# P times V in quarter-width tiles, a chain's items in a row, shift in place, 64-row mask products, merged constant loads, idle transposes first

## The reference

```python
q, k, v = (proj(Wq), proj(Wk), proj(Wv))
scores = einsum('bhsd,bhtd->bhst', q, k) * scale
scores = where(mask[None, None, :, :], -inf, scores)
out = einsum('bhst,bhtd->bhsd', softmax(scores), v).transpose(0, 2, 1, 3).reshape(B, S, E) @ Wo.T
xn = out / rms(out) * rms_scale
x = x + xn * (1.0 + sc[:, None, :]) + shift[:, None, :]      # sc, shift from silu(cond) @ Wc.T + bc
...
x = x + attention(g1 * x * inv_rms(x) + b1)                  # layer 1, no mask
x = x + (silu(n @ gate.T) * (n @ hid.T)) @ out_w.T           # n = g2 * x * inv_rms(x) + b2
```

## Time and profile before

| | |
|---|---|
| median of three runs | 370.43 us |
| profiled execution | 367.09 us |
| its span, first to last instruction | 365.3 us |
| TensorE matmul busy | 348.2 us, 95% |
| VectorE busy | 225.7 us, 62% |
| ScalarE busy | 216.0 us, 59% |
| GpSimd busy | 130.9 us, 36% |
| chain that ended last, by engine | PE 80%, DVE 7%, issue 3%, ACT 3% |

### The profile page before, as it was taken

How to read it: one execution, slowest core, us unless ns; L and a number is a source line. 1 busy time by engine, 2 the same in 40 slices (tenths; PEclk the granted TensorE clock), 3 DMA queues, 4 the chain that set the end, 5 groups by cost and what they waited for, 6 DMA issues and landing times.

```text
span 365.3 us, 10610 instructions
## 1 busy us (share of the span) xinstructions
PE 348.2 (95%) x4402; PEld 328.9 (90%) x4402; DVE 225.7 (62%) x361; ACT 216.0 (59%) x462; POOL 130.9 (36%) x146
## 2 busy tenths in 40 slices
PE   3899989899999999999999999999999999998995
PEld 3698889789999989998999999999999999998994
DVE  2377973979358878458356575766675765447241
ACT  4388878889866657256644647555684554442230
POOL 3005475953144213351037141334224216034422
PEclk9899999999999999999999999999999999999999
DMA  5738325300120000200020000000000000000001
GB/s 154 249 117 240 115 74 190 116 3 31 24 95 2 2 4 2 88 29 4 2 87 31 2 3 31 2 2 3 2 31 2 3 2 31 1 2 2 29 11 48
DMA packets 11919, 16.98 MB, mean 46 GB/s; under 512 B 1728, under 2 KB 6112, under 8 KB 11872
## 3 DMA queue, kind: packets, MB, share of 16 engines
q1 hardware_dynamic: 11872, 16.31, 14.2%
HBM read 14.14 MB, written 2.16 MB: 45 GB/s over the span
## 4 chain that ended last, share of the span: by engine, by line
PE 80%; DVE 7%; issue 3%; ACT 3%; SPq 2%; POOL 2%; DMA 1%; POOLq 0%; ACTq 0%; DVEq 0%
PE ps L1433 56%; PE ps L1531 8%; PE ps L1517 7%; PE ps L1507 4%; DVE row_max L1044 2%; PE ps L1542 2%; PE ps L1563 2%; PE ps L1496 2%; SPq L291 1%; DVE shifted L1052 1%; DVE xs_row L1097 1%; ACT v_pairs L594 1%; POOL h_lo L433 1%; DMA mask_u<-in_mask 1%; ACT probs L604 1%
## 5 line engine op out<-in xcount | busy, mean ns | idle before, releaser
L433 POOL TENSOR_TENSOR h_lo<-w_stage,h_hi 128x512 fp32r<-128x512 f32 x32 | 41.2, 1289 | 105.5 <-ACT h_hi L664 105.2
L1433 PE MATMUL ps<-ff_hi,w_hi 128*128 128x256 f32 x256 | 73.6, 288 | 0.1
L1433 PE MATMUL ps<-ff_hi,w_lo 128*128 128x256 f32 x256 | 72.1, 282 | 0.0
L1433 PE MATMUL ps<-ff_lo,w_hi 128*128 128x256 f32 x256 | 72.0, 281 | 0.0
L1044 DVE TENSOR_REDUCE row_max<-ps 128x8 f32<-128x512 f32 x64 | 43.7, 682 | 14.8 <-PE ps L1507 14.8
L604 ACT ACTIVATE probs<-shifted 128x512 f32<-128x512 f32 x64 | 39.4, 631 | 17.7 <-DVE shifted L1052 17.2
L1433 PEld LDWEIGHTS ps<-ff_hi,w_hi 128*128 128x128 f32 x256 | 48.2, 188 | 0.6 <-issue 0.5
L1433 PEld LDWEIGHTS ps<-ff_lo,w_hi 128*128 128x128 f32 x256 | 48.2, 188 | 0.0
L1433 PEld LDWEIGHTS ps<-ff_hi,w_lo 128*128 128x128 f32 x256 | 48.2, 188 | 0.0
L1433 PE MATMUL ps<-in_hi,w_hi 128*128 128x256 f32 x128 | 39.1, 306 | 6.5 <-DVE w_lo L1033 5.5
L1052 DVE SCALAR_TENSOR_TENSOR shifted<-row_max,ps 128x512 f32<-128x512 f32 x64 | 43.9, 687 | 2.2
(11 more groups left out here) (88 smaller groups left out, 803.6 us busy)
## 6 DMA issues: line engine op xcount, KB each, us to landing
w_stage<-in_weights SPq DMA_DIRECT2D x20, 256.0 KB, 3.4
mod_tile<-mod_rows_dram SPq DMA_DIRECT2D x32, 128.0 KB, 3.1
x_T<-in_xT SPq DMA_DIRECT2D x8, 256.0 KB, 2.7
x_row<-in_x SPq DMA_DIRECT2D x8, 256.0 KB, 2.8
out<-x SPq DMA_DIRECT2D x8, 256.0 KB, 2.2
x<-in_wcT SPq DMA_DIRECT2D x1, 128.0 KB, 2.9
x<-in_bc SPq DMA_DIRECT2D x1, 64.0 KB, 2.5
x<-in_g1wT SPq DMA_DIRECT2D x1, 64.0 KB, 2.2
```

What stands on the lines that cost most here:

```text
L433: pool.tensor_tensor(h_lo[q % 2][:], h_T[q % 2], h_hi[q % 2][:], ALU.subtract)\
L1433: mm = pe.matmul(dst, x, y, start=first and n == 0, stop=last and n == len(terms) - 1, skip_group_check=True)
```

## The change

- `weigh_values` issues, for each t and m, four products with 32 stationary columns (q = 0, 32, 64, 96) in place of two with 64. All other sizes stay.
- In the list of TensorE, the four items of a chain mostly stand in a row: 20 groups, twelve of four, two of three, four of two, two of one. All lists and all PSUM bank tables are new.
- `shift` writes into `probs`, and the exponential works in place; `shifted` is gone, `probs` has four buffers, `probs_T` five. A shift waits for the transposes four items back.
- The mask's matmuls use 64 rows of `mask_neg` and of a selector `sel_r` that puts row i to outputs i and i + 64; even r uses the lower rows, odd r the upper.
- The constants come in three loads and the mask in one; x_T of chunk 1 is loaded before k0, the mask before v0.
- TensorE begins with 18 transposes of the identity into a bank that `keys(0)` overwrites.

```diff
+WARM = 18
-NSHIFT, NPROB, NPT, NX1 = 3, 3, 3, 5
+NPROB, NPT, NX1 = 4, 5, 5
...
-                sp.dma_start(mask_u8[0:S], a_in["mask"]).then_inc(mask_landed, 16)
-                sp.dma_start(mask_u8[S:P], a_in["mask"]).then_inc(mask_landed, 16)
+                sp.dma_start(mask_u8[:], a_in["mask"]).then_inc(mask_landed, 16)
...
+                sp.dma_start(cond_in, a_in["cond"]).then_inc(consts_landed, 16)
+                sp.dma_start(rows_in, a_in["rows"].partition_broadcast(NB)).then_inc(consts_landed, 16)
+                sp.dma_start(modb[:], a_in["modb"]).then_inc(consts_landed, 16)
...
             load_xT(0)
+            load_xT(1)
             load_w("k0")
             load_w("q0")
             load_consts()
+            load_mask()
             load_w("v0")
             load_w("o0")
-            load_xT(1)
+            load_w("k1")
             load_xT(2)
-            load_mask()
...
-                wait(act, pT_ready, n - NPROB + 1)
-                act.activation(probs[n % NPROB][:], shifted[n % NSHIFT][:], ACT.Exp, scale=-SCALE)\
+                act.activation(probs[n % NPROB][:], probs[n % NPROB][:], ACT.Exp, scale=-SCALE)\
...
-                dve.tensor_copy(ident_r[:], ident[:]).then_inc(sel_ready, 1)
+                dve.tensor_tensor(sel_r[:], ident[:, 0:S].unsqueeze(1).to_broadcast([P, 2, S]),
+                                  ident[:, S:P].unsqueeze(1).to_broadcast([P, 2, S]), ALU.add).then_inc(sel_ready, 1)
...
-                wait(dve, probs_ready, n - NSHIFT + 1)
-                dve.scalar_tensor_tensor(out=shifted[n % NSHIFT][:].rearrange("p (g s) -> p g s", s=S),
+                wait(dve, pT_ready, n - NPROB + 1)
+                dve.scalar_tensor_tensor(out=probs[n % NPROB][:].rearrange("p (g s) -> p g s", s=S),
...
             set_up_parity()
             input_lo(0)
             weight_lo("k0")
+            set_up_mask()
             weight_lo("q0")
-            set_up_mask()
-            condition()
-            modT_in()
+            weight_lo("v0")
             input_lo(1)
...
+            def warm_up():
+
+                pe.wait_ge(ident_ready, 1)
+                for n in range(WARM):
+                    pe.transpose(ps[:, K_BANK[0], P * (n % 4):P * (n % 4) + P], ident[:], ident[:])
...
                     for r in range(NR):
-                        pe.matmul(ps[:, S_BANK[a][r], :], ident_r[:], mask_neg[:].rearrange("q g s -> q (g s)"),
+                        rows = slice(S * (r % 2), S * (r % 2) + S)
+                        pe.matmul(ps[:, S_BANK[a][r], :], sel_r[rows].rearrange("q b s -> q (b s)"),
+                                  mask_neg[rows].rearrange("q g s -> q (g s)"),
                                   start=True, stop=False, skip_group_check=True)
...
-                        for b in range(2):
-                            mm = pe.matmul(ps[S * b:S * b + S, OUT_BANK[a][t], 2 * DE * pr:2 * DE * (pr + 1)],
-                                           probs_T[n % NPT][:, at + S * b:at + S * b + S],
-                                           v_pairs[a % NS][:, t, b, pr, :], start=True, stop=True)
+                        for q in range(0, P, 32):
+                            mm = pe.matmul(ps[q:q + 32, OUT_BANK[a][t], 2 * DE * pr:2 * DE * (pr + 1)],
+                                           probs_T[n % NPT][:, at + q:at + q + 32],
+                                           v_pairs[a % NS][:, t, q // S, pr, :], start=True, stop=True)
```

More of the change, by code:

```diff
@@ L833, in _ @@
[L833 to L850 removed]
+            copy_pT(8, 3)
@@ L1661, in _ @@
+            output_product(3, oT_read(3))
+            transpose_probs(4, 1, pT_read(4, 0))
+            transpose_probs(4, 2, scores_read(4, 3))
+            transpose_normed(2, v_read(5))
+            transpose_probs(4, 3, y_read(3))
+            keys(6, pT_read(4, 1))
+            queries(6, xsT_read(2))
+            weigh_values(4, 0, pT_read(4, 3), scores_read(5, 0))
             weigh_values(4, 1)
-            transpose_output(3, scores_read(4, 3))
-            scores(5, pT_read(4, 1), pT_read(4, 2), out_read(3))
+            values(6, pT_read(4, 2))
@@ L1684, in _ @@
+            keys(7, xsT_read(3))
+            transpose_output(4, pT_read(5, 1))
+            scores(6, pT_read(5, 0), out_read(4), pT_read(5, 2))
+            transpose_probs(5, 3, scores_read(5, 3))
+            output_product(4, oT_read(4))
+            queries(7, k_read(7))
+            transpose_probs(6, 0, scores_read(6, 0))
+            values(7, pT_read(5, 3))
+            weigh_values(5, 0, scores_read(6, 1), scores_read(6, 2))
             weigh_values(5, 1)
@@ L1717, in _ @@
-            transpose_output(6, scores_read(7, 3))
             weigh_values(7, 1)
             weigh_values(7, 2)
-            scores(8, pT_read(7, 1), gu_read(0, 3), pT_read(7, 2))
-            transpose_probs(7, 3, oT_read(6))
+            weigh_values(7, 3)
+            hidden_in(0, 7)
+            scores(8, out_read(7), k_read(9), pT_read(7, 3))
+            transpose_output(7, y_read(6))
+            hidden_out(0, 1)
+            queries(9, gu_read(0, 3))
+            keys(10, gu_read(0, 3))
@@ L1747, in _ @@
-            values(9, y_read(7))
-            transpose_normed(7, acc_read(0))
-            queries(10, q_read(9))
-            weigh_values(8, 0, gu_read(1, 2))
-            values(10, v_read(9))
-            scores(9, gu_read(1, 3), pT_read(8, 3), xsT_read(7))
-            keys(11, q_read(10))
+            weigh_values(8, 0, scores_read(9, 0), scores_read(9, 1))
             weigh_values(8, 1)
@@ L1756, in _ @@
             weigh_values(8, 3)
[L1757 to L1764 removed]
+            hidden_out(0, 6)
+            hidden_in(1, 4, gu_read(1, 1))
+            hidden_out(0, 7)
@@ new lines, in _ @@
+            values(9, scores_read(9, 2))
+            hidden_in(1, 5)
+            transpose_probs(9, 1, scores_read(9, 3))
+            transpose_normed(7, out_read(8))
+            keys(11, out_read(8))
+            queries(10, v_read(9))
+            transpose_output(8, xsT_read(7))
+            transpose_probs(9, 2, pT_read(9, 1))
+            hidden_in(1, 6, gu_read(1, 2))
+            transpose_probs(9, 3, pT_read(9, 2))
+            output_product(8, acc_read(0))
+            scores(10, oT_read(8), k_read(11), pT_read(9, 0), q_read(10))
@@ new lines, in _ @@
+            hidden_out(2, 1)
+            queries(13, k_read(13))
+            hidden_out(2, 2)
+            hidden_in(3, 2, oT_read(11), scores_read(12, 2))
+            output_product(11, scores_read(12, 3))
+            hidden_out(2, 3)
+            transpose_probs(12, 1, pT_read(12, 0))
+            transpose_probs(12, 2, q_read(13))
+            hidden_out(2, 4)
+            scores(13, pT_read(12, 1), y_read(11), gu_read(3, 0))
+            transpose_probs(12, 3, pT_read(12, 2))
+            hidden_out(2, 5)
```

1286 lines of the change are left out of this document (615 added, 671 removed), and 18 rows, old and new, of tables (GU_BANK, S_BANK, T_BANK).

## The result

| | before | after |
|---|---|---|
| median, runs taken side by side | 369.85 us (4 runs) | 346.9 us (4 runs, 345.44 to 349.28) |
| ratio, 95% interval | | 0.9415 [0.9373, 0.9457] |
| profiled execution | 367.09 us | 349.28 us |
| its span | 365.3 us | 347.5 us |
| TensorE matmul busy | 348.2 us | 331.4 us |

The ratio is not the quotient of the two medians, which is 0.938. One execution of the kernel before, beside the run again, took 557 us at a granted clock of 0.56; the ratios leave it out.

The account below looks back on a forecast made before the run. It took TensorE's list of work as the bound from 99 to 328 us, with ScalarE pressing too before that. Terms -5.0 - 8.4 - 3.8 - 3.0 - 1.0 + 3.2 = -18.0 us, from median 370.43 to 352.4 us; range 345 to 362.

Parts of the forecast that it names:

- grouping: weigh_values order: 20 groups in place of 39, priced at 0.30 us each; 5.0 us less (bounds 4 and 5.7).
- quarter tiles: weigh_values in 32-column tiles: an item takes 0.335 in place of 0.467 us; 8.4 us less over 64 items.
- mask products: Mask matmuls of 64 rows run two side by side, four in 0.55 us; 3.8 us less (bounds 0 and 4.3).
- start: New load order and 18 transposes raising the clock: keys(1) at 13.7 in place of 18.44 us; 3.0 us less.
- end: Waits for h_lo and of transpose_normed(15) near the end covered by moved products; 1.0 us less together.
- waits given back: Before 99 us, half of TensorE's gain there returns as waiting; 3.2 us more (bounds 1.5 and 11).
- rival (a): Faster still: weigh_values items at the load bound (4.6 us less), little given back; about 346 us, chance 0.15.
- (d): weigh_values tile no cheaper: 0.467 us an item (361 us) or 17.8 ns a record (367.5 us); chance 0.11.
- (e): Slower: weigh_values price hangs on the record, 29.2 ns whatever the width; 391 us, chance 0.09.
- Rival (c): Half-height masks run one after another (3.8 us) and transposes don't raise the clock (2.5); 359 us, chance 0.10.
- Rival (b): Groups of four and a full ScalarE turn gains into waiting, 8 us more; 360 us, chance 0.13.

Follow-up runs that it names:

- again: The changed kernel once more, word for word: 346.64 us, ratio 0.9406.
- split: The changed kernel with nine groups of four in chains 7 to 15 broken up by full-array products, 13 groups more: 356.92 us, ratio 0.9659.
- wide64: The changed kernel with weigh_values back in 64-column tiles: 355.4 us, ratio 0.9648.
- mask128: The changed kernel with the mask products over the identity and all 128 rows again: 349.94 us, ratio 0.9473.
- move17: The changed kernel with 17 moving columns in place of 34 in weigh_values, plus two filling products a chain: 361.47 us.
- consts_late: The changed kernel with the three constant loads issued after k1 in place of before the mask: 344.56 us, ratio 0.9346.
- front2: The changed kernel with the three constant loads after k1 and x_T of chunk 1 loaded after v0: 342.06 us, ratio 0.9281.
- npt4: The changed kernel with four probs_T buffers in place of five: 346.0 us, ratio 0.9406.
- before_q32: The kernel before with only the 32-column tiles put into weigh_values: 364.31 us, ratio 0.9865.
- stat16: The changed kernel with 16 stationary columns in place of 32 in weigh_values, plus two filling products a chain: 358.93 us.
- warm0: The changed kernel without the 18 transposes at its head: 350.26 us, ratio 0.9484.

## Why the prediction was right, and where not

| step of the sum | forecast | measured |
|---|---|---|
| grouping | -5.0 | -4.9 in the list, 0.24 a group in split |
| quarter tiles | -8.4 | -11.5 in the list, -8.5 by wide64 |
| mask products | -3.8 | -2.9 in the list, -2 to -3 by mask128 |
| start | -3.0 | +3.2 in this execution |
| end | -1.0 | -2.3 |
| waits given back | +3.2 | +1.5 |
| sum | -18.0 | -17.6 (with 0.7 of the list unassigned); the spans differ by 17.8 |

**Right.** What bounds the kernel, and therefore the rule by which everything was priced: an edit is worth what it takes from TensorE's list. Distances from the chain of waits and not busy times carried over to the kernel after to 0.01 us for the group (0.12). TensorE stays nearly without gaps from 100 us to 310 us (0.22 us).

**Quarter tiles: the term was mis-sized, by its mechanism.** The item costs 0.29 us, not 0.335. The bounds were 0.26 and 0.57, and my value came from a window of 16 products refilled when the oldest is done. move17 speaks against such a window: shorter products were not refilled sooner. The price is 18 ns for an fp32 product, and neither fewer stationary nor fewer moving columns change it. The load bound of 0.26 (rival (a)) is not what binds either, though it lies close. Rivals (d) and (e) hung on a price of 17.8 and of 29.2 ns for each record; measured are 9 ns a record, half of the lower one. Both took over a record's price from another shape of tile, and it didn't carry over. Whether the record or the product is what is paid for, no run tells, since every fp32 product here is two records.

**Mask: mis-sized.** 0.66 in place of 0.55 us for four. The two halves overlap, but less than fully; I had taken the score tiles as the pattern.

**Start: the step that failed.** Its term was -3.0 us and came out as +3.2 in the profiled execution. The wrong sign belongs to that execution: with keys(1) at 17.59, the middle one of the nine traces, the term would be about +1, and with the earliest, 15.56, about -1, by an estimate from their distance to 19.77. What failed in all nine is the size. I let k0 land one tile later than before and the mask 3.2 us after its issue, as in the earlier trace rows. In after k0's conversion begins at 7.56 us and the mask needs until 12.06. The step took each transfer's latency from a place where the queue was short, and the change puts two x tiles, two weight blocks and nearly 500 KB of constants into it ahead of the mask. The DMA issues of after (KB each, median us from issue to landing) show how long that queue is:

```profile
x<-in_cond SPq DMA_DIRECT2D x1, 392.0 KB, 6.5
x<-in_rows SPq DMA_DIRECT2D x1, 96.0 KB, 7.4
```

consts_late and front2 show the cause by taking it away: without the constants ahead of the mask the median falls by 2.1 us (keys(1) 2.7 earlier), and without x_T of chunk 1 ahead of k0 by another 2.5 (keys(1) 3.6 earlier, part of it by the clock). The clock followed: I had read half clock behind idle out of the earlier trace rows, but my own idle times were short (1.1 us before keys(0), 1.2 before queries(0)), and those that came were up to 3.3 us. That short ones are harmless is not shown either, as wide64 and npt4 ran keys(0) at half clock behind 1.15 and 1.31 us. In front2, where there is no such idle time, the forecast of the start comes true and more (keys(1) at 11.91, forecast 13.7). Rival (c) priced this: half of it, transposes that bring no full clock, came true in the trace of after, where the 24 matmuls from 13.34 us on take 4.70 us in place of 2.85.

**End and waits: too cautious.** Behind 300 us 1.2 us of waits are left of 3.5; the h_lo wait stays (0.72 us) and those of result(6) and transpose_normed(15) are gone. The waits before 100 us grew by 1.2 and not by 3.2. That they could have grown by more is shown by before_q32: 5.8 us before 100 us, about 2 of them half clock and some 2.5 of the whole issue, and 2.2 behind it. Rival (b) thus comes close to the tile without the rest of the change. That it is the order which keeps it from coming true is likely, as npt4 finds the fifth buffer worth nothing, but it isn't shown.

**From the profiled execution to the median.** Here lies the whole 5.5 us by which the median missed. Between the profiled executions the gain is 17.8 us, between the medians 23 (beside again 21.7, with before at 368.3). The profiled execution of before was 3.3 us under its median, and I added these for the kernel after too; that of after was the slowest of four, 2.4 above. For after it is the start: with the same code keys(1) began at 18.27 us in again, in place of 19.77, and the span was 345.4; in npt4, with one buffer less, it was 16.27 and 343.3. For before it is the clock. Its profiled execution had a mean granted clock of 0.995, and 36 others on record line up by theirs:

| granted clock of before | executions | us |
|---|---|---|
| 0.995 | 12 | 367.36 to 367.90 |
| 0.990, 0.991 | 10 | 368.12 to 369.41 |
| 0.985, 0.986 | 13 | 369.86 to 370.75 |

(one more, 370.33 us, shows 0.94). From 0.995 to 0.986 is 0.009 of 368 us, 6.6 us more at half clock, worth at most 3.3 us where TensorE is busy, by an estimate; 2.6 were measured. So the 3.3 us that I carried over were mostly half clock, and the trace of after has a granted clock of 1.00. No trace of a slower execution of before says where in the span it lies; in before_q32, at 0.985, it was the stretch from 13.7 to 24 us. An offset between one execution and a median is no property that a change carries over; it belongs into the range, not into the sum.

## What to carry to other kernels

Price an edit of a saturated engine's order by distances from start to start in the chain of waits, and price a place in the order twice: for the change of kind that it causes, and for the latency of another engine that the work there hides. Compare the idle time that the profile puts down to issue, too: small edits moved it by 1 to 4 us here, and it is easily taken for the effect of the edit. A new first transfer pays for every byte queued ahead of it: sum the queue, don't carry a latency over from a place where it was short. Small tiles are worth having until the price hangs on the number of products; here that was 18 ns for an fp32 product on four column tiles, in each of three shapes up to 32 by 34 columns. And look at the granted clock of each execution before you call a difference of a median a property of the code.

## What the runs showed of the hardware

- Products of fp32 on four column tiles in turn, all 128 rows: 18 ns each from start to start (16 in 0.29 us), the same with 16 or 32 stationary and with 17 or 34 moving columns. With 64 stationary columns on two column tiles it was 58 ns (8 in 0.467).
- Transposes can raise TensorE's clock, in some executions while they still run. In mask128 the 18 lie as follows (duration ns min/median/max, first and last start; then the stretch with the first 13, columns as in the earlier trace rows):

```profile
L1437 PE MATMUL ps<-ident x18: 272/421/475, 1.5 to 4.8; 128*128 128x128 f32 x18
```

```profile
1.50:4.20 2.70, 2.68 (x13) 2.68 (x14) 0.34 (x2) 1.13 (x2) 2.42 (x6) 1.00 0.86 253
```

13 in 2.70 us are 0.21 apart; the other five begin between 4.2 and 4.8, 0.12 apart, and the shortest takes 272 ns, near the mean of 275 of the transposes of probs in after (at full clock). split is alike (18 in 3.52 us). In after, again, wide64, npt4 and stat16 all 18 stay 0.21 apart or nearly (4.10 us), and keys(0) behind them runs at full clock in again only. The granted clock of that stretch reads 1.00 although the distances are those of half clock; so at the very start the distances tell more than that column.

- The clock falls in the middle of the steady part too: warm0 had 3.40 us at half clock behind the stall shown above, with TensorE busy throughout:

```profile
191.90:195.30 3.40, 3.40 (x18) 3.40 (x18) 1.64 (x4) 1.15 (x2) 0.00 (x0) 0.50 0.02 5
```
